# The output projection's bias as a one-row product on TensorE instead of an addition on GpSimd

## The reference

```python
xn = _layernorm(x, norm_w, norm_b)
xz = xn @ in_proj_w.T + in_proj_b
xc, z = jnp.split(xz, 2, axis=-1)
...
y = _selective_scan(u, delta, A, B_ssm, C_ssm)
y = y + u * D_param
y = y * _silu(z)
out = y @ out_proj_w.T + out_proj_b
return residual + out
```

## Time and profile before

| | |
|---|---|
| median of 3 runs | 3536.71 us (3534.97 to 3543.54) |
| the profiled execution's own time | 3544.69 us |
| its span, first to last instruction | 3542.6 us |
| mean granted TensorE clock over it | 0.921 |
| GpSimd, the addition L758 | 16 times, 2357 ns each |
| VectorE, the addition of the result L1206 | 32 times |

### The profile page before, as it was taken

How to read it: one execution, slowest core, us unless ns; L and a number is a source line. 1 busy time by engine, 2 the same in 40 slices (tenths; PEclk the granted TensorE clock), 3 DMA queues, 4 the chain that set the end, 5 groups by cost and what they waited for, 6 DMA issues and landing times. The chain is left out here.

```text
span 3542.6 us, 46535 instructions
## 1 busy us (share of the span) xinstructions
PE 2906.6 (82%) x12696; PEld 1877.5 (53%) x12697; DVE 2575.6 (73%) x4149; ACT 2043.0 (58%) x3770; POOL 2601.8 (73%) x2481
## 2 busy tenths in 40 slices
PE   2776979797988888797979788888877679999997
PEld 1444555555555564555555555555454356666664
DVE  2498989899898989898999989898978312222221
ACT  2577667676766767767767667676654123333332
POOL 1389898888989898989899898989898223333333
PEclk8887989899999999898989999999887789999998
DMA  2001111111111011111111110101111243333332
GB/s 71 19 31 33 34 42 38 38 40 37 45 34 48 28 50 32 45 34 42 40 38 38 40 48 28 51 29 41 34 42 39 73 110 54 54 53 54 53 51 43
DMA packets 113256, 155.35 MB, mean 44 GB/s; under 512 B 15600, under 2 KB 72368, under 8 KB 113072
## 3 DMA queue, kind: packets, MB, share of 16 engines
q1 hardware_dynamic: 72624, 99.79, 9.6%
q0 software_dynamic: 26112, 35.81, 5.9%
q10 hardware_dynamic: 14336, 17.57, 1.5%
HBM read 107.36 MB, written 45.76 MB: 43 GB/s over the span
## 5 line engine op out<-in xcount | busy, mean ns | idle before, releaser
L810 POOL TENSOR_TENSOR dbu<-du,bbc 128x512 f32<-128x512 f32 x1024 | 1296.2, 1282 | 112.6 <-DVE h L1328 106.2
L1328 DVE TENSOR_TENSOR_SCAN h<-bank,dbu 128x512 f32<-128x512 f32 x1024 | 1225.4, 1210 | 153.7 <-ACT bank L1012 94.2
L1012 ACT ACTIVATE bank<-delta,amat 128x512 f32<-128x512 f32 x1024 | 703.3, 691 | 319.3 <-DVE h L1328 306.6
L638 PE MATMUL bank<-ident,h 128*128 128x128 f32 x4096 | 629.4, 290 | 266.0 <-DVE acc L1318 236.2
L638 PEld LDWEIGHTS bank<-ident,h 128*128 128x128 f32 x4096 | 500.5, 149 | 554.1 <-DVE acc L1318 219.7
L796 POOL TENSOR_TENSOR acc<-acc,hTc 128x512 f32<-128x512 f32 x480 | 610.1, 1271 | 97.8 <-ACT hTc L996 95.4
L1531 POOL DMA_INDIRECT out<-ye,ids x136 | 213.7, 1571 | 450.2 <-issue 236.9
L996 ACT ACTIVATE hTc<-bank,cT 128x512 f32<-128x512 f32 x480 | 327.1, 682 | 252.5 <-PE bank L638 252.2
L1578 DVE SCALAR_TENSOR_TENSOR gg<-gt,bank 128x352 f32<-128x352 f32 x136 | 70.9, 522 | 499.9 <-ACT gt L1481 499.9
L1318 DVE SCALAR_TENSOR_TENSOR acc<-bank,cT,acc 128x512 f32<-128x512 f32 x544 | 394.1, 729 | 40.5 <-PE bank L638 38.7
L592 PE MATMUL bank<-x4T,w_su 128*128 128x512 f32 (+1 forms) x768 | 395.5, 619 | 10.7 <-DVE score L1227 10.7
(11 more groups left out here) (200 smaller groups left out, 4382.3 us busy)
## 6 DMA issues: line engine op xcount, KB each, us to landing
bbc<-b_scratch SPq DMA_DIRECT2D x256, 256.0 KB, 3.1
xe<-slots_in SPq DMA_DIRECT2D x136, 129.0 KB
x<-in_x SPq DMA_DIRECT2D x16, 512.0 KB, 3.9
out<-x ACTq DMA_DIRECT2D x16, 512.0 KB, 2.9
w_gu<-in_e_gu ACTq DMA_DIRECT2D x8, 704.0 KB
out<-ye,ids POOLq DMA_INDIRECT x136, 3.8
slots_in<-x,pos POOLq DMA_INDIRECT x128
w_dn<-in_e_dn ACTq DMA_DIRECT2D x16, 128.0 KB
```

Of the source, the lines that this page charges most:

```text
L638: last = tr(scan[f"hT{s}.{t}"][:, m * P:(m + 1) * P], h[:, s % 2, m, t * P:(t + 1) * P], ident[:, :])
L810: g.tensor_tensor(dbu[:, n % 4, :], du[:, m, :], bbc[:, (b * NS + s) % NROW, :], ALU.mult).then_inc(S("dbu_ready"), 1)
L1012: f(db(n)[:, :], delta[:, par, m, :], ACT.Exp, scale=amat[:, m, s:s + 1]).then_inc(S("da_ready"), 1)
L1328: v.tensor_tensor_scan(h[:, s % 2, m, :], db(n)[:, :], dbu[:, n % 4, :], 0.0, ALU.mult, ALU.add)\
```

## The change

For every tile, TensorE starts the accumulation with a product of one row: a row of ones (`ones_p[0:1]`, 128 long) times the bias (`out_b[0:1]`, 256 columns); the four products with `w_out` then accumulate on it. GpSimd's addition is taken out, with its slot in the table and its semaphore. VectorE's first L1206 waits for `res_ready` (ScalarE) instead of `base_ready` (GpSimd). The wait for the constants `tri` and `ones_p` goes from the count of the router to the first output projection; it occurs once.

```diff
@@ TensorE, late_of
                     if k == 0:
                         done(pe, "y3_ready", b)
+                        if b == 0:
+                            pe.wait_ge(tri_ready, 1)
                     late.may_fill(pe, f"out{k}", b, done)
                     for j in (2 * k, 2 * k + 1):
                         if j % 2:
                             yield AT["out"][k] + 1
+                        result = late[f"out{k}", b][:, (j % 2) * D:(j % 2 + 1) * D]
+                        mm(result, ones_p[0:1, :], out_b[0:1, :], start=True, stop=False)
                         for m in range(MC):
-                            last = mm(late[f"out{k}", b][:, (j % 2) * D:(j % 2 + 1) * D], zs[:, par, m, j * P:(j + 1) * P], w_out[:, m, :],
-                                      start=m == 0, stop=m == MC - 1)
+                            last = mm(result, zs[:, par, m, j * P:(j + 1) * P], w_out[:, m, :], start=False, stop=m == MC - 1)
@@ TensorE, count_of
                     late.may_fill(pe, "count", b, done)
-                    if b == 0:
-                        pe.wait_ge(tri_ready, 1)
@@ GpSimd, projections_of
-                yield AT["base"]
-                done(pool, "res_ready", b)
-                g.tensor_tensor(x2[:, b % NX2, :, :], x2[:, b % NX2, :, :], out_b[:, :].unsqueeze(1).broadcast_to([P, TT, D]), ALU.add)\
-                    .then_inc(S("base_ready"), 1)
@@ VectorE, late_of
                     if k == 0:
-                        done(dve, "base_ready", b)
+                        done(dve, "res_ready", b)
```

More of the change, by code:

```diff
@@ L255, in layers @@
                    inv_ready=1, probT_ready=TT, x1_ready=2, xb_ready=1, q_ready=1, qT_ready=1, yb_ready=2, yb2_ready=1,
-                   x2_ready=1, res_ready=1, base_ready=1, r4_ready=1, r4T_ready=DC, zh_ready=MC,
+                   x2_ready=1, res_ready=1, r4_ready=1, r4T_ready=DC, zh_ready=MC,
                    zt_ready=MC, zs_ready=MC, conv_first=MC, conv_tap=MC * (TAPS - 1), conv_ready=MC, conv_tanh=MC,
@@ L298, in layers @@
             stats3=2, rstd3=1, res=3, r4=4, r4T_pe=5, r4T=3, in_x=(8, 10, 15, 17), tap=(11, 12, 17, 19), conv=(13, 15, 19, 21),
-            tanh=(13, 15, 20, 21), u=(16, 17, 23, 24), base=12, xBC_pe=24, bs=25, cT_pe=29, cT=31, in_z=(31, 38, 45, 51),
+            tanh=(13, 15, 20, 21), u=(16, 17, 23, 24), xBC_pe=24, bs=25, cT_pe=29, cT=31, in_z=(31, 38, 45, 51),
             z=(33, 40, 48, 53), zs=(38, 43, 50, 55), dt_pe=(26, 34, 40, 49), raw=(30, 38, 44, 52), sp_exp=(32, 44, 49, 55), sp_ln=51,
```

## The result

The changed kernel takes 3560.07 us (median of 6 runs, 3558.4 to 3561.05) against 3534.98 us for the kernel before (median of 6, 3529.2 to 3543.54). The ratio is 1.0069, interval 1.0056 to 1.0082. I had forecast 3543.9 with a range of 3532 to 3557, so the change costs 25.1 us where I gave it 7.2, and the result lies outside the range.

A forecast was written before the change was run, and what follows sets the result against it. VectorE's scan, with GpSimd close behind, was taken to bound the turns, through which wait ends last. 5.5 us in the turns plus 1.7 at the end made 7.2 on the median 3536.7: 3543.9 us, range 3532 to 3557.

The forecast's parts named there:

- Part 1: GpSimd's addition L758 goes, 37.7 us less GpSimd work; VectorE's own work hides it, so gain 0.
- Part 2, the price: Four one-row products per sequence on TensorE at 0.43 us each, 28 us more work; upper end 0.86 us each.
- Part 2, the readers' room: TensorE runs 1.2 us late from 991.21 to 1003 in turn 5; its readers there were assumed to have room.
- Part 3, what the lateness meets: VectorE, 0.3 us late, meets GpSimd without its addition; about 0.4 us per turn stays, 5.5 us in all.
- the wait at the scores: VectorE's wait of 0.84 us for TensorE's scores at L1102, to absorb most of a lateness of up to 1.4 us.
- the detour: VectorE's second tiny addition L1162 just misses GpSimd's change of instruction and pays about 1.1 us.
- Part 4, the end: Late part of sequence 15, with nothing beside it: all four products on the path, 1.7 us, at most 3.4.
- The clock falls out of step: Rival: turns 4 to 13 go at the pace of turns 1 to 3, 14 us more, 3558; chance 0.24.
- All absorbed: Rival: the one-row product is cheap or L1102's wait takes everything; only the end remains, 3538.5; chance 0.18.
- GpSimd's release: Rival: VectorE's tiny additions find relieved GpSimd idle, 19 us gained less the 7, 3525; chance 0.08.

The follow-up runs named there:

- the removal alone: The changed kernel without the one-row bias products, so the bias is left out altogether and GpSimd's addition stays gone; 3533.36 us, ratio 0.9982.
- all rows: The changed kernel with the bias product over all 128 rows instead of one, the bias divided by 128; 3555.38 us, ratio 1.0036.
- the early full kernel: The changed kernel with the bias products moved to the turn's start, two of 512 columns over all 128 rows; 3532.47 us, ratio 0.9971.

## Why the prediction was wrong
**Part 1, GpSimd's addition: right for the settled turns.** 38.6 us less work, gain nothing there (163.85 in the kernel without it). The gain of 0 for the whole kernel was too low: the removal alone has a ratio of 0.9982, and its profile is shorter in turns 0 and 14 by 5.6 and 3.3 us. The prediction had the 5.72 us of turn 0 in its rows, and used them as a danger only.

**Part 2, the price: the step that failed.** "I take 0.43: the product has the 256 columns of its neighbours, and the row that it is nearest to is theirs." It measured 0.85 us, beside the upper end of 0.86 that I had given for another reason, the clock. The row that it was nearest to was not L552 but L604, a product with fewer rows than those around it, whose idle stands in the view of the weight loads. With 0.85 the prediction's own formula gives 2 x 0.85 - 0.55 = 1.15 us of lateness per turn; the rows show 1.2 at the seventh scan. Room, order of events and the one who waits were right, the wait was 4.03 us and not 3.1. Fourteen turns at 1.15 and 1.5 at the end make 17.6 us, 3554.3: the price explains most of the miss, but not all.

**Part 2, the readers' room: right at the price taken, gone at the price paid.** It was marked as an assumption. With full-row products in the places of the change no addition of VectorE in that stretch waits; with one-row products an addition to `acc` waits 0.28 us, which takes the lateness from 1.2 to 1.5 us on the way to the tiny addition.

**Part 3, what the lateness meets: the wait at the scores right, the detour not.** In the changed kernel the second tiny addition takes 1.23 us (0.18 before), the wait at the scores is eaten up, the third takes 0.6 us less. From 1.2 us late, that leaves 1.1, in the three turns that keep in step. But the forecast had the detour at 0.3 us late. With all rows, where the lateness was 0.4, the second tiny addition took 0.32 us and not 1.1, and the wait at the scores went from 0.84 to 0.55 and took the lateness down to 0.23.

**Part 4, the end: 1.5 us for 1.7,** by luck in part: the price was double, and the stretch had no 1.2 GHz this time.

**The rivals.** *The clock falls out of step* is what happened, with the number I gave it (3558 for all turns; measured 3560). It came about otherwise than priced, though: 11 of the 21 us in turns 4 to 13 are plain lateness, and 10 are the clock in part of the turns. **This is the second step that failed, and it would have failed at the right price too:** with full-row products at 0.43 us the seventh scan is late as forecast, and the ratios are still 1.0036 and 1.0045, 13 and 16 us and not 7. I had argued that the turns "settled by themselves" and that a shift would be half given back. Both are so, but there is little room for it: in the kernel before, the fall of the clock rests 1.36 to 1.39 us ahead of the turn, and the long turns begin at 1.50. With all rows a turn is still 0.06 us too long when it gets there, and every second or third turn falls into the long cold stretch and loses 3 us. The 0.3 to 0.4 us per turn of the forecast should have been set against these 0.1 us or so. *All absorbed* would have been right with one product ahead of L487 (ratio 1.0006). *GpSimd's release* did nothing to the tiny addition that it named, which took 0.91 to 0.92 us in most turns without GpSimd's addition too; what turns 0 and 14 gained came elsewhere.

What stays open: why the clock falls as it does at the start of a turn and not in the early full kernel. Also whether the lateness alone makes the turns slip: every kernel that slips has more TensorE work than the one before, and none delays a turn without adding any. For the lateness speaks that the four kernels with full-row products at the projection have their products in different places and one edge: where the fall comes 1.51 us or more ahead of one of turns 4 to 13, the long stretch follows, and at 1.49 or less it never does. And why the runs of the kernel before spread over 20 us. In its profile turn 7 starts with the clock's fall 1.49 us ahead, 0.01 to 0.02 from where others slipped, and one slip costs 3 us, so slips now and then could explain part of the spread, the tiny addition of turn 0 (5.7 us) and the part behind the scans (8 us over the profiles) more of it; but no profiles of a short and a long run of it were set side by side.

## What to carry to other kernels
Price a TensorE product by the loads around it: look for idle "issue" time ahead of weight loads in the view by form, and don't set products of one or 64 rows among those of 128; a one-row operand can be spread over all rows with its values scaled down. Where turns repeat in step with the granted clock, ask not only how large a new lateness is but how much of it the next turns give back, and how far the nearest long turn lies, for a few tenths of a us can end in a slip of 3 us. Extra work for TensorE belongs where it waits for somebody else, ahead of the stretch in which somebody waits for it.

## What the runs showed of the hardware
- A weight load of 1 or 64 rows behind one of 128 rows, or of 128 behind one of 1 or 64, comes after 0.33 us of idle (0.17 for the former behind a state transpose); 128 behind 128 and 96 behind 128 come after 0.03 us. In float32, a product of 256 columns so costs 0.85 us with one row or 64, and 0.33 to 0.43 with 128.
- The same turn, with the same code, lasts 163.9 to 164.1 or 167.0 us in the kernel with all rows (one of turns 4 to 13 164.4), with 6.8 or 10.2 us at 1.2 GHz at its start.
- With a full-row product of 1.02 us put into the start of a turn, the clock there was 1.00 in nine of turns 4 to 13, where it was 0.50 without it; with a one-row product in the same place it was not.
- The tiny addition of VectorE on three columns took 0.18, 0.33, 0.92 or 1.23 us, and 5.72 in turn 0 of the kernel before. That one ends at 202.51, when five instructions of GpSimd, the last at 201.21 for 1.27 us, have ended.
